# Three neighbour sums of a graph kernel: node work for four node tiles at once in place of at every pair

## The reference, cut to what matters

```python
def _gcn_norm(edge_index, n_nodes):
    ...                                     # loops added, deg = edges that end at a node
    deg_inv_sqrt = jnp.where(deg > 0, jax.lax.rsqrt(deg), 0.0)
    norm = deg_inv_sqrt[src] * deg_inv_sqrt[dst]
def _gcn_conv(x, src, dst, norm, W, b, n_nodes):
    h = x @ W
    msg = h[src] * norm[:, None]
    out = jax.ops.segment_sum(msg, dst, num_segments=n_nodes)
    return out + b
h = relu(_gcn_conv(h, ..., W1, b1)); h = relu(_gcn_conv(h, ..., W2, b2)); h = relu(_gcn_conv(h, ..., W3, b3))
```

## Time and profile before

| | us |
|---|---|
| runs, median (lowest, highest) | 17,230.35 (17,207.27, 17,251.48) |
| profiled execution: its span (the page has no other time for it) | 17,231.0 |
| busy: PE / PE weight load / DVE / ACT / POOL | 6403.2 / 4040.9 / 7021.0 / 2781.2 / 9553.7 |
| gathers of sum0 | 501.3 to 2839.5 |
| gathers of sum1 | 2877.5 to 5493.4 |
| gathers of sum2 | 5546.9 to 7945.4 |

### The profile page before, as it was taken

The page is one execution under the profiler, slowest core; times in us unless marked ns, Lnnn a source line. Parts: engine busy times, 40 slices in busy tenths (PEclk is TensorE's granted clock), DMA queues, the critical chain, the costliest instruction groups (busy, mean ns, idle before and its releaser), DMA issues. The chain is left out here.

```text
span 17231.0 us, 133710 instructions
## 1 busy us (share of the span) xinstructions
PE 6403.2 (37%) x28658; PEld 4040.9 (23%) x28659; DVE 7021.0 (41%) x15685; ACT 2781.2 (16%) x4350; POOL 9553.7 (55%) x9902
## 2 busy tenths in 40 slices
PE   4212222444444112212122222466566656344446
PEld 1111111222222111111011111222222226232234
DVE  6322222222222233333366667666666652232232
ACT  1112212444444111111000001000000001000001
POOL 0566666555555666664666664355454551666663
PEclk9555555666666555555555555688888875666665
DMA  2111111222221111112233332222222222111111
GB/s 88 25 24 26 25 25 40 62 60 61 60 61 49 18 19 19 19 19 83 70 86 88 88 87 73 49 56 57 55 57 55 57 59 56 19 20 20 19 20 47
DMA packets 761665, 826.94 MB, mean 48 GB/s; under 512 B 353366, under 2 KB 526785, under 8 KB 758438
## 3 DMA queue, kind: packets, MB, share of 16 engines
q0 software_dynamic: 340624, 383.65, 12.0%
q1 hardware_dynamic: 271806, 297.17, 5.7%
q10 hardware_dynamic: 148312, 136.41, 2.8%
HBM read 657.66 MB, written 158.81 MB: 47 GB/s over the span
## 5 line engine op out<-in xcount | busy, mean ns | idle before, releaser
L736 POOL DMA_INDIRECT rel_ring<-scratch_tab,k_src x1664 | 1583.0, 951 | 1557.0 <-DVE rel_message L2281 1033.7
L675 PE MATMUL rel_accumulator<-rel_message,rel_onehot 128*128 128x512 f32 x3328 | 1762.1, 678 | 1203.1 <-DVE rel_message L2281 968.4
L1229 POOL DMA_INDIRECT sum0g_ring<-scratch_parts,k_group_src x1568 | 1558.7, 994 | 1098.5 <-issue 479.7
L1229 POOL DMA_INDIRECT sum1g_ring<-scratch_parts,k_group_src x1568 | 1531.9, 977 | 1122.0 <-SPq L1243 622.0
L736 POOL DMA_INDIRECT pass_ring<-scratch_tab,k_src x1664 | 1654.6, 994 | 867.4 <-issue 486.1
L736 POOL DMA_INDIRECT sh_ring<-scratch_tab,k_src x1664 | 1569.9, 943 | 939.2 <-issue 495.7
L1229 POOL DMA_INDIRECT sum2g_ring<-scratch_parts,k_group_src x1568 | 1518.4, 968 | 933.6 <-issue 466.2
L675 PE MATMUL sh_accumulator<-sh_message,sh_onehot 128*128 128x248 f32 x3328 | 1055.1, 446 | 1444.8 <-issue 1407.7
L675 PEld LDWEIGHTS sh_accumulator<-sh_message,sh_onehot 128*128 128x128 f32 x3328 | 750.2, 228 | 1749.1 <-issue 1681.3
L675 PEld LDWEIGHTS rel_accumulator<-rel_message,rel_onehot 128*128 128x128 f32 x3328 | 684.1, 217 | 1991.7 <-issue 1991.6
L2281 DVE TENSOR_TENSOR rel_message<-numbers,rel_ring 128x2048 f32<-128x2048 f32 x416 | 953.0, 2291 | 14.3
(11 more groups left out here) (435 smaller groups left out, 14437.8 us busy)
## 6 DMA issues: line engine op xcount, KB each, us to landing
rel_rel_rows<-scratch_rel_rows ACTq DMA_DIRECT2D x211, 256.0 KB
pass_rows<-scratch_rel_rows SPq DMA_DIRECT2D x208, 256.0 KB
scratch_kv<-pass_ring SPq DMA_DIRECT2D x208, 256.0 KB
pass_kept<-scratch_kv SPq DMA_DIRECT2D x208, 256.0 KB
rel_type_rows<-scratch_type_rows ACTq DMA_DIRECT2D x211, 172.0 KB
rel_ring<-scratch_tab,k_src POOLq DMA_INDIRECT x1672
pass_ring<-scratch_tab,k_src POOLq DMA_INDIRECT x1664
sh_ring<-scratch_tab,k_src POOLq DMA_INDIRECT x1664
```

The lines of the kernel that those rows point to most:

```text
L675: self.nc.tensor.matmul(self.accumulator[:, bass.ds(self.banks[g], self.width)], onehot, rows, start=False, stop=True, skip_group_check=Tr ...
L736: nc.gpsimd.indirect_dma_start(out=ring[:, q, g, :], out_offset=None, in_=table, in_offset=bass.IndirectOffsetOnAxis(ap=k["src"][:, n * G ...
L1229: nc.gpsimd.indirect_dma_start(out=ring[:, n % slots, g, :], out_offset=None, in_=table, in_offset=bass.IndirectOffsetOnAxis(ap=k["group_s ...
```

## The change

A pair now only folds its sum into the row of its node tile in a table for all nodes (`sums`, `wide`, `own`), which begins with the nodes' own rows; the sum carried from pair to pair, `keep` and `dinv_pair` go. Node work is done for four node tiles at once (25 quads). Quad b may be touched last by pair `min(98 - 1 + 4b + 3, 195)`, since each pair moves on by at least one of group and node tile; its node work stands behind that pair, at a lag. So the first quad is due at pair 100, one more every four pairs, and pairs 0 to 99 have no node work. W1 and the query/key/value weights are block-diagonal for four node tiles (32 rows each); in sum1 W2 is the stationary operand and its result comes out transposed, so the second transpose goes. The numbers of node tiles and slots are loaded for eight pairs at once; the slot has a word row of its own. `copy_rows` and the other waits of `Gathered` drop the offset of 16 and the waits on pairs before the first.

In the shared part:

```diff
+def _due(n, lag):
+    for b in range(QUADS):
+        if _complete(b) + lag == n:
+            yield b
+def _complete(b):
+    return min(NG - 1 + QUAD * b + QUAD - 1, NS - 1)
...
-        dve.wait_ge(self.multiplied, m - 3 + BASE)
+        if m >= 4:
+            dve.wait_ge(self.multiplied, m - 3)
...
-        pe.wait_ge(self.folded, m - 3 + BASE)
+        if m >= 4:
+            pe.wait_ge(self.folded, 2 * (m - 4) + 1)
...
-    def fold(self, dve, k, m):
+    def fold(self, dve, words, m, sums):
         q = m % 2
-        dve.wait_ge(self.multiplied, m + 1 + BASE)
-        self.nc.vector.tensor_reduce(self.joined[q][:], self.totals[:, m % 4, 0:3 * self.width].rearrange("p (c f) -> p f c", c=3),
-                                     axis=AX_X, op=ALU.add).then_inc(self.folding, 1)
-        dve.wait_ge(self.folding, m + 1)
-        self.nc.vector.scalar_tensor_tensor(out=self.sums[q][:], in0=self.sums[1 - q][:], scalar=k["keep"][:, m:m + 1],
-                                            in1=self.joined[q][:], op0=ALU.mult, op1=ALU.add).then_inc(self.folded, 1)
-        dve.wait_ge(self.folded, m + 1 + BASE)
-    def begin(self, dve):
-        self.nc.vector.memset(self.sums[1][:], 0.0)
-        dve.sem_inc(self.folded, BASE)
+        tile = words.at(m)
+        dve.wait_ge(self.multiplied, m + 1)
+        self.nc.vector.tensor_reduce(self.joined[q][:], self.totals[:, m % 4, 0:self.held].rearrange("p (c f) -> p f c", c=3),
+                                     axis=AX_X, op=ALU.add).then_inc(self.folded, 1)
+        dve.wait_ge(self.folded, 2 * m + 1)
+        self.nc.vector.tensor_tensor(_tile(sums, tile), _tile(sums, tile), self.joined[q][:], ALU.add).then_inc(self.folded, 1)
+    def summed_up(self, dve, b):
+        dve.wait_ge(self.folded, 2 * _complete(b) + 2)
```

In `first_sums`, the node work of a quad (transpose and copy are left out) and ScalarE's list:

```diff
-        got = Gathered(nc, ctx, "sum0g", D, 4, 4, 2)
+        got = Gathered(nc, ctx, "sum0g", D, 4, 2, mark=1, lent=(k["q"], k["x_next"]))
...
+        def scale(dve, b):
+            tiles = _tiles_in(b)
+            n = tiles.stop - tiles.start
+            got.summed_up(dve, b)
+            if b >= 2:
+                dve.wait_ge(flipped, b - 1)
+            nc.vector.tensor_tensor(scaled[b % 2][:, 0:n, :], sums[:, tiles, 0:D],
+                                    k["dinv"][:, tiles].unsqueeze(2).to_broadcast([P, n, D]), ALU.mult).then_inc(scaled_sem, 1)
...
+        def mix(pe, b):
+            n = _tiles_in(b).stop - _tiles_in(b).start
+            pe.wait_ge(turned_sem, b + 1)
+            if b >= 1:
+                pe.wait_ge(raised, b)
+            nc.tensor.matmul(linear_ps[:, 0:n * HID], k["ones"][0:1, :], b1[0:1, 0:n * HID], start=True, stop=False)
+            nc.tensor.matmul(linear_ps[:, 0:n * HID], turned[b % 2][0:n * D, :], w1[0:n * D, 0:n, :].rearrange("p j f -> p (j f)"),
+                             start=False, stop=True).then_inc(mixed, 1)
...
+        def split_rows(dve, b):
+            tiles = _tiles_in(b)
+            n = tiles.stop - tiles.start
+            high, middle, low = (parts[b % 2][:, 0:n, c * HID:(c + 1) * HID] for c in range(3))
+            left = rest[:, 0:n, :]
+            dve.wait_ge(mixed, b + 1)
+            nc.vector.scalar_tensor_tensor(out=wide[:, tiles, :], in0=linear_ps[:, 0:n * HID].rearrange("p (j f) -> p j f", f=HID), scalar=0.0,
+                                           in1=k["dinv"][:, tiles].unsqueeze(2).to_broadcast([P, n, HID]), op0=ALU.max, op1=ALU.mult).then_inc(raised, 1)
+            if b >= 2:
+                dve.wait_ge(stored, (b - 1) * DMA)
+            dve.wait_ge(raised, b + 1)
+            _linked(dve, splitting, 3 * b + 1, nc.vector.tensor_copy(high, wide[:, tiles, :]))
+            _linked(dve, splitting, 3 * b + 2, nc.vector.tensor_tensor(left, wide[:, tiles, :], high, ALU.subtract))
+            _linked(dve, splitting, 3 * b + 3, nc.vector.tensor_copy(middle, left))
+            nc.vector.tensor_tensor(low, left, middle, ALU.subtract).then_inc(split, 1)
...
-                places = Places(nc, act, k)
-                def body(n, q):
-                    if _live(n, 0):
-                        got.copy_rows(act, places, n, k["marks"])
-                    if _live(n, 4):
-                        if n == 4:
-                            act.wait_ge(ready, 1)
-                        turn(act, n - 4, (n - 4) % 4)
-                    if _live(n, 5):
-                        activate(act, n - 5, (n - 5) % 4)
-                    if _live(n, 7):
-                        store(act, places, n - 7, (n - 7) % 4)
-                _pairs(body, 7)
-                act.wait_ge(stored, (NS + BASE) * DMA)
+                words = got.words_of_rows(act, k)
+                for n in range(NS + 9):
+                    if n < NS:
+                        got.copy_rows(act, words, n, k["marks"])
+                    for b in _due(n, 5):
+                        turn(act, b)
+                    for b in _due(n, 9):
+                        store(act, b)
+                act.wait_ge(stored, QUADS * DMA)
```

ScalarE's list in `second_sums` (VectorE's and TensorE's go the same way) and VectorE's in `third_sums`:

```diff
+                words = got.words_of_rows(act, k)
+                for n in range(NS + 10):
+                    if n < NS:
+                        got.copy_rows(act, words, n)
+                    for b in _due(n, 5):
+                        turn(act, b)
+                    for b in _due(n, 6):
+                        activate(act, b)
+                    for b in _due(n, 10):
+                        store(act, b)
...
+                for n in range(NS + 7):
+                    if n < NS:
                         got.make_one_hot(dve, k, n)
-                    if _live(n, 4):
-                        normalize(dve, places, n - 4, (n - 4) % 4)
-                    if _live(n, 3):
-                        add_own(dve, places, n - 3, (n - 3) % 4)
-                    if _live(n, 6):
-                        take_query(dve, places, n - 6, (n - 6) % 4)
-                _pairs(body, 6)
+                    if 0 <= n - 3 < NS:
+                        got.fold(dve, words, n - 3, own)
+                    for b in _due(n, 4):
+                        normalize(dve, b)
+                    for b in _due(n, 3):
+                        center(dve, b)
+                    for b in _due(n, 7):
+                        take_query(dve, b)
```

In `gcn_weights`, 24 DMAs (eight, then these sixteen behind two memsets) in place of nine:

```diff
+        blocks = []
+        for q in range(QUAD):
+            at = slice(q * D, (q + 1) * D)
+            blocks.append((w["w1"][at, q, :], io["L0_gnn_W1"]))
+            blocks += [(w["qkv"][at, q, c * D:(c + 1) * D], io[f"L1_gnn_W{n}"]) for c, n in enumerate("qkv")]
...
+                with nc.allow_non_contiguous_dma("a bias by partition"):
+                    for to, of in rows:
+                        sp.dma_start(to, of).then_inc(loaded, DMA)
+                sp.wait_ge(cleared, 2)
+                for to, of in blocks:
+                    sp.dma_start(to, of).then_inc(loaded, DMA)
+                sp.wait_ge(loaded, (len(rows) + len(blocks)) * DMA)
```

More of the change, by code:

```diff
@@ L756, in group_tables @@
         step = sb("step", [P, 4, 2])
[L757 to L759 removed]
+        words = sb("words", [1, WORDS, 2 * P])
         shift = sb("shift", [P, 2 * P])
@@ L1397, in first_sums, with store @@
+        def store(act, b):
+            tiles = _tiles_in(b)
+            act.wait_ge(split, b + 1)
+            if b >= 1:
+                act.wait_ge(stored, b * DMA)
+            act.dma_start(_node_rows(dram["parts128"], tiles.start, tiles.stop),
+                          parts[b % 2][:, 0:tiles.stop - tiles.start, :]).then_inc(stored, DMA)
         with nc.Block() as block:
```

648 lines of the change are left out of this document (298 added, 350 removed).

## The result

The changed kernel takes 16,759.6 us (median of four runs, 16,739.25 to 16,794.42) against 17,226.7 (four runs) of the kernel before: a ratio of 0.9725, 95% interval 0.9711 to 0.9739, or 467 us less. The profiled executions were 17,231.0 and 16,792.7 us, 438.3 apart, and what follows adds up that difference (the changed kernel's is the slowest of its four).

A forecast was written before the change was run, and what follows sets the result against it. It took GpSimd's gathers and their waits for ring slots as the bound. Terms: sum1 −188, sum2 −70, sum0 −15, between stages −10, weights +7, in sum −276 from 17,231 to 16,955 us; range 16,600 to 17,240.

The forecast's parts named there:

- the likeliest case: Whole kernel: the terms for stages, gaps and weights summed to 16,955 us, own range 16,830 to 17,090, chance 0.52.
- slow flow: Neighbour-sum stages: while gathers run unbroken, other engines' instructions slow, a VectorE link taking 1.39 us against 0.23.
- second rival: Whole kernel: little gain, VectorE being mostly idle and each stop backlog plus ScalarE's copies; 17,208 us, chance 0.14.
- The backlog as a floor: Each neighbour-sum stage: 0.155 us of backlog per gather, 243 us that no relief of VectorE removes; floor 2203 us.
- first rival: Three stages: fewer linked instructions also end the backlog; 15,893 us with every wait gone, 16,560 with half, chance 0.18.
- the term of −15: sum0: shorter pairs, 3.18 to 2.0 and 2.9 us, cut 58 us of catching up; −15, bounds +25 and −135.
- sum1's term: sum1: 4 us less in each of 47 GpSimd waits for a ring slot; −188 us, bounds 0 and −385.
- the nearest row says −60: sum2: sum0, with the same gathers and slots, takes 2338.2 us against 2398.4, so −60; −70 was taken.
- One more copy done at a stop: sum1: ScalarE's freed list lets one more 5.31 us copy finish before a stop; 4 us a wait, −188.
- VectorE's cadence: sum2: fewer VectorE instructions bring a pair from 4.96 us to 2.0 in the first half, 3.0 after; −70.
- Between stages: Tails behind each stage's last gather: shorter pairs save a few us from each of three; −10, bounds −25 and +10.
- third rival: Three stages: shorter pairs give denser gathers, more backlog and longer stops, so slower; 17,298 us, chance 0.10.

The follow-up runs named there:

- space: Changed kernel plus a GpSimd memset behind every second gather of sum0 and every gather of sum2; slow chip, 16,780.9 us.
- pad: Changed kernel plus linked VectorE dummies behind each fold, as many as the change took from a pair; 14,015.5 us quiet chip, 16,713.0 slow.
- tie: Changed kernel, but each copy of rows waits for the multiply two pairs back in all three stages; 14,004.8 us quiet chip, 16,668.1 slow.
- pad_tie: Changed kernel with both VectorE's dummies and the copy's wait for the multiply two pairs back; quiet chip, 14,020.9 us.
- Hot: Changed kernel with the one-hot's first operand read from PSUM instead of SBUF; slow chip, 16,870.1 us, ratio to the kernel before 0.9795.
- free: Changed kernel without sum2's pairs, slots released as soon as landed; quiet chip, sum2 stage 1956.4 us.

## Why the prediction was right, and where not

**The gain and its place: right, its size too small.** 16,955 us were forecast and 16,760 measured, within 16,600 to 17,240, but 70 us below the likeliest case's own range: a gain of 276 us against 467. All of it lies in the three stages and the gaps behind them.

**The slow flow: right, and the run on the quiet chip is what shows it.** The same change, with its 19,744 instructions fewer, brings no gain without the slow flow but a loss of 19 us. So the gain is not work saved. It is stops saved, and only where the slow flow is were there stops. That also speaks to the second rival (VectorE mostly idle, so nothing to win): it is exactly what happens on a chip without it. The reason for giving it only 0.14, the trace at hand, was a reason about one kind of chip.

**The backlog as a floor: right.** 0.155 us a gather was forecast, from a cost of "about 1.40". The count over the stops above and the run space put it at 1.40 us a gather. The first rival, that fewer linked instructions also end the pauses, is out: with less than half of VectorE's links left the pause behind a long run is still there, as long as the count says. I had the floor at 2203 us a stage; sum0 and sum2 are now 70 and 60 us above it. What the prediction had wrong is where the floor lies within the waits. It took 243 us of sum0's 300.8 as backlog, reckoned from gathers 1.25 us apart. Stretched by one-hots they were 1.30 apart and owed less, 158 us, so 143 and not 58 us were catching up, and the term of −15 was sized on the smaller number.

**What a stop costs: right in kind, wrong in form.** The prediction took sum1's term as 47 waits of 4 us less each. The profile after has 27 waits of 13.5 us: the waits kept their length and 20 of them are gone. By the split above this is because a stop pays backlog for all gathers in front of it and then catches up once; when more groups come free in one quick stretch, the next stop is later. The mean run (1568 gathers over one more than the stops) grew from 33 to 56 gathers in sum1 and from 36 to 87 in sum2. The sizes: sum1 −188 forecast, −234 measured; sum2 −70, −136; sum0 −15, −65. For sum2 the step that failed is "the nearest row says −60": it let sum2 come down to what sum0 has now, though sum0 itself was to gain by the same shorter pairs. A neighbour's time was taken as the measure where the catching up, 203 us of sum2, was the better one.

**The cause of sum1's term: mostly wrong.** "One more copy done at a stop" was to be 188 us. The prediction's own sign against it came: sum1's waits stayed above 12 us each. Nor did the stops hold fewer copies: of sum1's stops of over 4 us before, 24 saw one copy of rows start, 20 two and one three; after, 9, 9 and 8. Giving the copy its old tie back costs 49 of 234 us, or 20. So that step holds for a fifth or less.

**VectorE's cadence: mostly wrong.** For sum2 the term rests on a pair of 4.96 us becoming 2.0 in the first half and 3.0 in the second. It became 1.64 where no quad is due (one-hots at 5769.64, 5771.27 and 5772.91), so the size of the shortening was more than met. But dummies that restore the length give back 22 of 136 us (36 by the other measure). Something else of the old pair holds the rest. Its node work went from VectorE through TensorE and ScalarE and back, over six semaphores a pair in sum0, nine in sum1 and eight in sum2, and its transposes, small copies and products stood in the lists of all three engines, between one pair's multiply and the next. pad's dummies stand in VectorE's list alone, and tie restores one wait of the copy; neither the transposes and small copies nor the two together were restored on a slow chip (pad_tie ran on the quiet one). That about 100 us of sum2 and 185 of sum1 lie there is what is left over, not what was shown.

**Between stages: too small.** −10 forecast with a bound of −25, −57 measured, 38 of them behind sum2, whose pairs had the longest lists. **Weights: right in size:** fifteen more loads at 0.47 us; +7 was forecast, and the first gather was 12 us later on one chip and 4.7 on the quiet one.

**The third rival (slower by denser gathers)** did not come on the slow chips. Hot points to its mechanism, though does not isolate it: gathers that nothing stretches meet more stops and the stages grow. The side remark that fewer operations would free some 20 us of gathers a stage did not come: what the gathers of over 1045 ns held above 945 each went from 77, 43 and 39 us to 66, 65 and 78. On the quiet chip the changed kernel is slower by another way, one-hots that hit more gathers in sum1 (39 to 95 us) and sum2 (56 to 76).

## What to carry to other kernels

When an engine is a quarter busy and still late, look at the spacing of its instructions, not at its busy share: a load and a product that take 0.15 us and come 2.8 us apart have a bound that no list of work shows. If a stop pays for all that ran before it, split its length into what was owed and what is catching up; here only the second was won, by fewer stops and by shorter catching up. And time a change on more than one chip before believing a per cent: this one is worth −2.7% where the slow flow is and +0.14% where it isn't.

## What was not expected of the hardware

- The same program takes 13,978 to 13,987, 17,036 or 17,202 us by the chip it is on. The start of the program (first gather at 501 to 515 us) is alike on all; what differs is what runs beside indirect gathers, behind the three stages too (the relational pass's gathers span 2132.6 us quiet and 3133.8 slow, in the kernel before). The work that is held up comes later: beside the 98 gathers of `rl_current`, which take 121 us on both, TensorE does 80 products slow and 539 quiet, and from there to the next gather it is 333 us against 216.
- In the slow flow instructions start in steps of 0.70 us. Of 919 gaps of over 0.4 us between starts of TensorE's loads and products in sum2 of the changed kernel, 542 are 1.38 to 1.42 us, 144 are 0.68 to 0.72 and 39 are 2.08 to 2.12.
- What the 1.40 us are spent on stays open. One mark goes with it: the traces of slow chips hold 54,000 to 63,000 semaphore updates, those of the quiet chip 205,000 to 220,000, for the same programs. The loss too begins with the gathers: up to 500 us the kernel before keeps 1,761 on a slow chip and 1,740 on the quiet one. Either the slow flow and the loss of these records have one cause, or recording them is itself what the engines wait for; all runs listed here come with spans and clocks, so no run tells the two apart, and the gain is shown for such executions only.
- A one-hot of two SBUF operands stretches a gather beside it from 0.94 to as much as 2.0 us. With its first operand in PSUM no gather is stretched past 1.24 us. The Trainium skill ("SBUF — State Buffer", Who interferes with whom) says that a VectorE instruction with two SBUF inputs contends with a GpSimd instruction that reads SBUF. A gather reads its row numbers there (`k_group_src`), and free and hot agree. On a slow chip the stretch shows no cost: hot, without it, was not faster, as a stretched gather owes less when GpSimd stops.
